# A state-space layer with a gated feed-forward: W_out centred on ScalarE, the first block's gates beside column 0, and the last V product behind the output projection

## The reference, cut to what matters

```python
x = x_in                                             # (4, 2048, 256)
xn = layernorm(x)
xz = xn @ W_in;  xs, z = xz[..., :256], xz[..., 256:]
proj = xs @ W_x                                      # 256 + 16 + 16 columns
delta = softplus(proj[..., :256] @ W_dt + b_dt);  B, C = proj[..., 256:272], proj[..., 272:]
h_t[d, n] = exp(delta * -exp(A_log))[d, n] * h_{t-1}[d, n] + delta * xs * B[n]     # 16 states n
y = sum_n h_t[d, n] * C[n] + xs * D_param
y = (y * silu(z)) @ W_out + xn;  x = x + layernorm(y) * ln_g + ln_b
hn = layernorm(x)                                    # second half
r = sigmoid(mix(hn, mu_r) @ W_r.T);  k = relu(mix(hn, mu_k) @ W_k.T)**2
out = x + r * (k @ W_v.T)                            # mix: each token with the one before it
```

## Time and profile before

| what | value |
|---|---|
| median of 3 runs | 954.0 us (952.21 to 954.55) |
| profiled execution, its own time | 952.36 us |
| its span | 950.6 us |
| DVE busy | 906.0 us (95%) |
| POOL busy | 891.1 us (94%) |
| PE busy | 866.8 us (91%) |
| ACT busy | 846.4 us (89%) |
| granted TensorE clock, mean | 0.971 |

### The profile page before, as it was taken

The page is one execution under the profiler, slowest core; times in us unless marked ns, Lnnn a source line. Parts: engine busy times, 40 slices in busy tenths (PEclk is TensorE's granted clock), DMA queues, the critical chain, the costliest instruction groups (busy, mean ns, idle before and its releaser), DMA issues.

```text
span 950.6 us, 15856 instructions
## 1 busy us (share of the span) xinstructions
PE 866.8 (91%) x5030; PEld 688.3 (72%) x5030; DVE 906.0 (95%) x989; ACT 846.4 (89%) x2058; POOL 891.1 (94%) x400
## 2 busy tenths in 40 slices
PE   8665688999999899999999899998999899999997
PEld 4345476867878687887868678786778768788885
DVE  4999999999999999999999999999999999999876
ACT  4586889999999899998999999998999999988865
POOL 3899999999999989999999989999999999999970
PEclk9878999999999999999999999999999999999999
DMA  7443555463544635454463634446354444535221
GB/s 217 153 167 127 199 199 190 149 237 140 184 159 180 239 147 185 181 176 159 178 241 149 224 147 170 166 178 246 148 185 180 177 163 173 201 144 191 102 88 44
DMA packets 49938, 163.60 MB, mean 172 GB/s; under 512 B 5248, under 2 KB 33152, under 8 KB 33600
## 3 DMA queue, kind: packets, MB, share of 16 engines
q1 hardware_dynamic: 48528, 161.27, 45.9%
q0 software_dynamic: 512, 1.31, 0.5%
q10 hardware_dynamic: 816, 0.02, 0.1%
HBM read 153.15 MB, written 9.44 MB: 171 GB/s over the span
## 4 chain that ended last, share of the span: by engine, by line
PE 48%; ACT 28%; DVE 14%; issue 9%; DMA 1%; SPq 0%; DVEq 0%; ACTq 0%
PE w_ps L1321 11%; PE y_ps L1312 10%; ACT da_ps L649 10%; PE w_ps L1345 6%; PE w_ps L1354 5%; PE w_ps L1357 5%; DVE da_ps L1027 4%; DVE hg L1043 3%; PE w_ps L1459 3%; DVE hg L1027 2%; PE w_ps L1363 2%; DVE hg L1034 2%; ACT xn_tok L588 2%; ACT h_tok L588 2%; ACT zs L710 1%
## 5 line engine op out<-in xcount | busy, mean ns | idle before, releaser
L539 POOL TENSOR_TENSOR dbx<-u,b_ring 128x1024 f32<-128x1024 f32 x255 | 599.0, 2378 | 8.5 <-DVE hg L1027 5.7
L649 ACT ACTIVATE da_ps<-delta,a_neg 128x512 f32<-128x512 f32 x512 | 340.5, 685 | 22.5 <-DVE hg L1034 7.1
L552 POOL TENSOR_TENSOR hg<-hg,c_ring 128x1024 f32<-128x1024 f32 x123 | 292.4, 2378 | 6.7 <-ACT carry L655 6.3
L1312 PE MATMUL y_ps<-ident,hg 128*128 128x128 f32 x2048 | 262.4, 278 | 10.7 <-POOL hg L552 10.7
L1312 PEld LDWEIGHTS y_ps<-ident,hg 128*128 128x128 f32 x2048 | 240.4, 144 | 37.4 <-issue 17.5
L1027 DVE TENSOR_TENSOR_SCAN da_ps<-da_ps,carry,dbx 128x512 f32<-128x512 f32 x201 | 247.5, 1273 | 2.9 <-ACT da_ps L649 2.9
L1027 DVE TENSOR_TENSOR_SCAN hg<-da_ps,carry,dbx 128x512 f32<-128x512 f32 x183 | 222.8, 1266 | 1.7 <-ACT carry L655 1.2
L1034 DVE TENSOR_TENSOR hg<-da_ps,c_ring 128x1024 f32<-128x1024 f32 x68 | 82.5, 1213 | 0.2
L1043 DVE TENSOR_TENSOR hg<-da_ps,c_ring 128x512 f32<-128x512 f32 x128 | 81.1, 676 | 0.0
L1027 DVE TENSOR_TENSOR_SCAN da_ps<-da_ps,dbx 128x512 f32<-128x512 f32 x64 | 75.6, 1213 | 3.0 <-ACT da_ps L649 2.9
L1321 PE MATMUL w_ps<-xnT_ring,w_in 128*128 128x512 f32 x120 | 61.7, 638 | 16.2 <-ACT xT L691 14.1
(11 more groups left out here) (207 smaller groups left out, 1341.9 us busy)
## 6 DMA issues: line engine op xcount, KB each, us to landing
c_ring<-bc_rows_dram SPq DMA_DIRECT2D x64, 1024.0 KB, 4.7
b_ring<-bc_rows_dram SPq DMA_DIRECT2D x63, 1024.0 KB, 6.7
xres<-in_L_attn_x_in_dram SPq DMA_DIRECT2D x16, 512.0 KB, 4.7
x_tok<-in_L_attn_x_in_dram SPq DMA_DIRECT2D x15, 512.0 KB, 6.0
out_dram<-r_out SPq DMA_DIRECT2D x15, 512.0 KB, 3.2
bc_rows_dram<-bc_rows SPq DMA_DIRECT2D x64, 16.0 KB, 5.5
w_in<-in_L_attn_W_in_dram SPq DMA_DIRECT2D x2, 256.0 KB, 4.3
x_tok<-in_L_attn_x_in_dram SPq DMA_DIRECT2D x2, 256.0 KB, 4.7
```

The lines of the kernel that those rows point to most:

```text
L539: pool.tensor_tensor(dbx[:, n % X_RING, :, :], u[:, ip, :, :], b.to_broadcast([P, KH, LC]), ALU.mult).then_inc(s["dbx_done"], 1)
L552: pool.tensor_tensor(part, part, c_of(n).to_broadcast([P, KH, LC]), ALU.mult).then_inc(s["g_pool"], 1)
L649: act.activation(da_of(n, h), delta[:, ip, h, :], ACT.Exp, scale=a_neg[:, h, n:n + 1]).then_inc(s["da_ready"], 1)
L1312: last = pe.matmul(y_tok[:, b, h * P:(h + 1) * P], hg[:, n % H_RING, h, b * P:(b + 1) * P], ident[:, :], is_transpose=True, start=n == 0 a ...
```

## The change

It does five things.

1. `center_w_out` leaves VectorE. ScalarE does it at place 6 of step 0: two Copy instructions scaled by -1/256 with an accumulator output give minus the mean, two Identity instructions add it.
2. The first block's `tanh_z` goes from place 2 to place 0 of step 0, its `silu` from place 3 to place 1, which is ahead of the scan of column 1.
3. The head's tables are new (the diff shows ScalarE's; the order below shows the others). On TensorE the broadcast of B's column 0 moves ahead of the `x1` product, that of column 1 ahead of the turning of W_k and W_v. On ScalarE `da` of column 0 is a stage of its own (`da0`), ahead of `xT`. On VectorE `scale_ffn_weight` of W_k and W_v moves behind column 0's scan.
4. `late_v0` and `late_v1` leave step 7. In `close()` they take the place of the dummy products in front of and behind `h_turned(0)`; `out_late` moves behind block 7's first `mix` pair; r of block 6 and its output are kept in `x_tok`, and the store is issued in `close()`.
5. `LAST_SPLIT` gets column 12: VectorE instead of GpSimd multiplies it with C.

```diff
-LAST_SPLIT = [5, 6, 8, 9, 11]
+LAST_SPLIT = [5, 6, 8, 9, 11, 12]
-ACT_HEAD = dict(xnT0=2, xnT1=9, bc=9, sp0=9, sp1=10, rsq1=24, x1=25, col0=26, x0=28, col1=31)
+ACT_HEAD = dict(xnT0=0, xnT1=0, bc=2, sp0=4, sp1=6, rsq1=7, col0=8, da0=9, x0=10, x1=12, col1=13)
...
@@ exps
-                    need_all_read(act, -1, [unit for unit in HEAD_UNITS if unit[0] != "z"])
+                    need_all_read(act, -1, ["dt0", "dt1"])
                     act.wait_ge(s["a_set"], 1)
+                elif i == 0 and n == 1:
+                    need_all_read(act, -1, ["x0", "x1"])
...
-                    if t == 0 and place == 2:
+                    if t == 0 and place == 0:
                         act.preload_act_table_set(EXP_TANH)
                         for m in range(2):
                             tanh_z(-1, m, par)
...
+                    if t == 0 and place == 6:
+                        for k in range(KH):
+                            act.activation(spare[:, k, :], w_out[:, k, :], ACT.Copy, scale=-1.0 / D,
+                                           accum_out=w_mean[k]).then_inc(s["w_out_set"], 1)
+                        for k in range(KH):
+                            act.wait_ge(s["w_out_set"], KH)
+                            act.activation(w_out[:, k, :], w_out[:, k, :], ACT.Identity,
+                                           bias=w_mean[k]).then_inc(s["w_out_set"], 1)
...
-                    if t == 0 and place == 3:
+                    if t == 0 and place == 1:
                         for m in range(2):
                             silu(-1, m, par)
-                        center_w_out()
...
@@ turn_ffn_weight, first_column
-                if m < 2:
-                    pe.wait_ge(s["setup_ev"], 2 + m)
+                if m == 0:
+                    pe.wait_ge(s["setup_ev"], 2)
                 else:
-                    pe.wait_ge(s["b_begun"], 1)
+                    pe.wait_ge(s["b_begun"], 3 - m)
...
@@ close() on TensorE
                 def k_of(v):
                     pe.wait_ge(last_mix[v], 1)
+                    if v == 1:
+                        pe.wait_ge(late_out, 2)
...
                 def v_of(v):
                     pe.wait_ge(last_kact[v], 1)
+                    if v == 0:
+                        pe.wait_ge(late_out, 1)
...
+                def late_v(v):
+                    need(pe, s["kact_done"], LAST)
+                    by_token(V_LATE[v], v, kact, w_vT).then_inc(late_v_done, 1)
...
-                keep_busy(work[1], 2)
+                late_v(0)
                 h_turned(0)
-                keep_busy(work[1], 1)
+                late_v(1)
                 k_of(0)
```

More of the change, by code:

```diff
@@ L178, in mamba_rwkv_layer @@
         r_out = sb("r_out", P, TB, D)
-        w_stats = [gated[:, 1, 128 + 6 * k:134 + 6 * k] for k in range(KH)]
-        w_mean = [gated[:, 1, 144 + 2 * k:146 + 2 * k] for k in range(KH)]
+        w_mean = [gated[:, 1, 144 + 2 * k:145 + 2 * k] for k in range(KH)]
         W_LOADS = 4
@@ L221, in mamba_rwkv_layer @@
         last_y = sem("last_y")
+        late_v_done, late_out = sem("late_v_done"), sem("late_out")
         (last_gated, last_turned, last_kept, last_wo, last_sq, last_lv2, last_rs2, last_g, last_x2, last_bn, last_mean,
@@ L240, in mamba_rwkv_layer @@
         END = [unit for unit in UNITS if unit[:-1] in ("hT", "r", "k", "v")]
-        LATE = ["late_" + unit for unit in END]
+        LATE = ["late_" + unit for unit in END if unit[0] != "v"]
         PRE = [unit for unit in UNITS if unit not in MID + END]
@@ L478, in step @@
                 for mark, c in ended(t, end, late):
-                    for v in range(2):
-                        need_read(sp, t, f"{mark}v{v}")
-                    sp.dma_start(out_v[c], r_out[:, :, :]).then_inc(s["out_stored"], 16)
+                    if c < LAST - 1:
+                        for v in range(2):
+                            need_read(sp, t, f"{mark}v{v}")
+                        sp.dma_start(out_v[c], r_out[:, :, :]).then_inc(s["out_stored"], 16)
                     if late and c == LAST - 2:
@@ L487, in close @@
             def close():
+                sp.wait_ge(late_out, 2)
+                sp.dma_start(out_v[LAST - 1], x_tok[:, :, :]).then_inc(s["out_stored"], 16)
                 sp.wait_ge(last_out[0], 1)
@@ L726, in step @@
                         keep_split_carry(t, n)
-                    if ahead:
+                    if ahead and not start:
                         exps(*ahead, half)
@@ L805, in step @@
                         act.preload_act_table_set(LN_EXP)
+                    if start and at("da0"):
+                        for h in range(KH):
+                            exps(0, nxt, 0, h)
                     if start and at("rsq1"):
@@ L1108, in step @@
                         first_moments(1)
-                    for m in range(3):
-                        if start and at(f"ffn{m}"):
-                            scale_ffn_weight(m)
+                    if start and at("ffn0"):
+                        scale_ffn_weight(0)
+                    if t == 0 and place == 0:
+                        scale_ffn_weight(1)
+                        scale_ffn_weight(2)
                     if start and at("norm"):
@@ L1158, in out_late @@
                     need(dve, ln_sum[3], LAST)
-                    dve.tensor_tensor(part, b, xres[:, 1 - par, 2 * v:2 * v + 2, :], ALU.add).then_inc(read_sem(LAST, f"late_v{v}"), 1)
+                    dve.tensor_tensor(part, b, xres[:, 1 - par, 2 * v:2 * v + 2, :], ALU.add).then_inc(late_out, 1)
                 def bias_added():
@@ L1229, in close @@
                 gate(1)
-                out_late(0)
-                out_late(1)
                 bias_added()
@@ L1242, in close @@
                 mix(0, h_of, mur, 2)
+                out_late(0)
+                out_late(1)
                 mix(1, xk, muk, 1)
```

50 lines of the change are left out of this document (21 added, 29 removed).

## The result

The changed kernel takes **942.28 us** (median of 4 runs, 941.48 to 943.15) where the kernel before takes 953.11 beside it: a ratio of 0.9888, 95% interval 0.9876 to 0.9900.

A forecast was written before the change was run, and what follows sets the result against it. Bound by chains of waits at both ends, not by one engine's average. Head 5.5 plus tail 3.15 (3.45 - 0.3) make 8.65 us; 954.0 - 8.65 = 945.4, range 942.6 to 949.6.

The forecast's parts named there:

- Column 0: Head: earlier broadcast starts GpSimd at 21.5 instead of 23.65, its first full product at 25.2, 1.1 us earlier.
- The gate: Head, first block: tanh and silu end at about 31.3; column 1's scan waits for that, column 2 follows at 33.6.
- the rival of the late gate: Head: TensorE's pauses let its clock fall; head gains only 1 to 4 us, 947 to 950; chance 0.19.
- GpSimd's track: Head: eight instructions without idle from 25.2; column 3's product with C at 43.8 instead of 49.29, 5.5 us earlier.
- the three waits: Head: GpSimd's `dbx` waits for column 2's scan and its followers, 2.58, 1.05 and 0.70 us, expected to go.
- the 4.33 us of waits: Head: sum of GpSimd's waits for scans queued behind VectorE's operations on `w_out`, counted as gained.
- Centring on ScalarE: Head, between column 4's `da` halves: 1.8 us and hidden; upper price 4.19, which would make `carry` 1.3 us late.
- The tail: Last block: gate 3.45 us earlier without V products ahead of it, less 0.3 given back behind it: 3.15.
- The middle: Steps between head and tail: passes on the head's gain and shifts as a whole, with no gain of its own.
- More than I see, a wait of the middle: Middle: a wait there goes with the shift, giving a time under 942.6; chance 0.05.
- the slower case: Middle: each of seven block changes gets a 1.7 us GpSimd wait for `carry`, 12 us in all: 957.3; chance 0.06.
- a close at 0: Behind the last gate: bounds of 0 to 1 us for the cost of the work moved into `close()`; 0.3 taken.

The follow-up runs named there:

- silu-at-column-3 kernel: Changed kernel with the first block's tanh and silu back at columns 2 and 3, centring left on ScalarE: 948.93 us, ratio 0.9962.
- The two kernels with half of it: Changed kernel with the centring back on VectorE, 949.58 us; changed kernel with the first block's tanh and silu back at columns 2 and 3, 948.93 us.
- taking only that away: Kernel before with only the centring of W_out moved to ScalarE: 951.94 us, ratio 0.9986.
- the next two: The changed kernel run twice more, unchanged: 943.47 us (ratio 0.9903) and 943.44 us (ratio 0.9885).
- head alone: Kernel before with parts 1 to 3 and two 512-column products ahead of each block's first turning (one in step 1): 942.02 us.
- both ends, start filled: Changed kernel with two products ahead of each first turning, plus two 256-column products in the setup at the very start: 939.66 us, ratio 0.9848.
- both ends, with the turning of 1.37: Changed kernel with two 512-column products ahead of each block's first turning (one in step 1): 939.81 us, ratio 0.9866.
- the head alone: Kernel before with parts 1 to 3 of the change, tail as before: 946.37 us, ratio 0.9932.
- the tail alone: Kernel before with parts 4 and 5 of the change, two memset flags joined into one: 950.41 us, ratio 0.9972.

## Where the prediction went wrong, and what of it held

*Column 0.* Forecast 21.5 for GpSimd's first product, 23.9 for the second, 25.2 for the first full one; measured 21.28, 23.64, 24.86. Of the 0.3, 0.2 were there at the first turning of x (11.82 for 12.03), a matter of that execution. Right.

*The gate.* Forecast: done at 31.3, column 2 at 33.6, dummies at 31.3 with 3.5 us, clock 1.00. Measured 30.8, 33.01, 31.20 with 3.67, and 1.00. Right, and the rival of the late gate fell with it. The silu-at-column-3 kernel shows that a longer pause does cost the head: there the idle time ahead of the dummies was 4.39, they took 2.5 us more, and nearly the whole head was lost.

*GpSimd's track.* Right in form: the three waits are gone and eight instructions fill the time; 5.94 us gained for 5.5. The two kernels with half of it show that it needs both edits. The prediction put the 4.33 us of waits down to VectorE's centring alone; taking only that away gave 0.1, since block 1's turned input held ScalarE's exponentials as long. It drew that path (ScalarE's 5.39 us of idle) but gave it no price.

*Centring on ScalarE.* 1.8 us, as taken, and hidden. That VectorE's two operations take 4.2 to 4.9 beside GpSimd was seen again with the centring back on VectorE. The Trainium skill ("SBUF — State Buffer", "Who interferes with whom") states that a two-port form of VectorE and GpSimd shut each other out for a whole instruction; these rows agree with it.

*The tail.* 3.14 at the gate for 3.45, 0.2 given back for 0.3. TensorE waited 0.20 for GpSimd's last half, so the two close together, as drawn, and 0.3 later. `out_late` put the third `mix` 0.3 late for the 0.4 that was drawn. Right.

*The middle.* This is the step that failed: "What the head gives GpSimd, the middle therefore passes on; it shifts as a whole", costed at 0. The middle is not a fixed length: in the stretches above a long turning adds 0.6 to 1.2 us, and the profiled execution of before had two where the changed kernel's had none. So the middle gave 1.7 in the first pair of traces, -1.1 and +0.3 in the next two against the same trace of before. As far as these traces tell, the 1.7 is the chance of these two executions and no effect of the change. With the two products ahead of the turnings, against the kernel before with them, the stretch from gate 0 to gate 14 gives 0.7 (head alone), 0.65 (both ends, start filled) and -0.25 (both ends, with the turning of 1.37). Of the first, 0.4 lies between gates 0 and 1; around there GpSimd's `dbx` products take 2.425 us in the mean in the kernel before with the products and 2.387 in the head-only one. That is not shown to be the cause: between gates 2 and 3 they take 2.52 and 2.39, and the stretch has the same length within 0.01. Whether anything of the middle belongs to the change stays open.

*The sum.* In the first pair of traces the terms are 6.05, 1.7 and 2.9 where the forecast had 5.5, 0 and 3.15, so the middle is the term that was missed. By medians against the pooled 953.04, the head alone gives 6.7, the tail alone 2.6 and both 9.8. Against 942.28 itself, 3.1 were missing: the base, 954.0 from three runs, lies 1.0 above the median of 67; 0.9 is the distance of that first median from the changed kernel's own over twelve runs; the other 1.2 are the terms. "More than I see, a wait of the middle" was given 0.05 and no place, though the trace of before already had a wait of TensorE for `xn_tok` in every block. The first median fell into that case's range, but not for its reason, since the waits that were missing were not tied to the shift. That it lies outside the forecast's range is partly luck: the changed kernel's pooled 943.23 lies inside.

*The range and the slower case.* The lower bound of 942.6 doesn't follow from the bounds beside it: a head of 5.5 and a close at 0 give 954.0 - 5.5 - 3.45 = 945.05, and nothing was named for the 2.4 below. The slower case was sized with seven block changes; with fifteen, 1.7 us each make 25.5 us, and it would have decided from 0.6 us a change on. It didn't come: GpSimd's waits for `carry` went from 6.3 to 5.6.

## What to carry to other kernels

When a wait is on the path, look for who would release it next before pricing its removal: here the same 4.3 us had two releasers on different engines, and without either edit at most 1.3 us of the head's 6 were left. Where TensorE idles a couple of microseconds once in every block, read the first instruction behind it in each block: if some of them take twice as long, a product that fits into the gap, sized by a row of that kernel and not longer, is worth more than its cost (3 to 4 us here), and products that don't fit cost 2 to 3. Forecast from a median over many runs, and from two traces of the kernel before where one is at hand; a pair of single traces put the same gate of the same kernel up to 3.8 us apart here.

## What the runs showed of the hardware

- TensorE's turnings ran long (1.31 to 1.94 us for 1.06), with a granted clock of 0.50 to 0.77 over the 5 or 6 us around those that were looked at, behind idle times of only 1.1 to 3.1 us, in some blocks of an execution and not in others, with the same code and idle time (2.12 us ahead of 306.64 and 306.66: 1.94 and 1.06). With some 1.9 us of products in the gap and 0.2 to 0.6 us of idle left, no turning took over 1.10 in any of four traces from 140 us on. The Trainium skill ("TensorE: Matmul & The Clock Gate", "What's actually happening") has the low level as the default that activity releases; these falls behind idle time agree.
- The first products of an execution ran at about half speed for a time that differs: the same one took 3.78 or 1.99 us at a reported granted clock of 1.00, and put the whole kernel 2 us later.
- ScalarE's 128x256 copy with accumulator and its biased form took 0.40 and about 0.45 us beside a busy GpSimd, VectorE's form 1.8 to 2.5.
